# Keeping the four upper rows of a strip in place, and summing normalised tokens in GpSimd first

## What is computed

```python
# layer 0: windows of 8x8 queries against 12x12 keys (a halo of 2 pixels), 6 heads of 16
x = x + conv0(ln_c(x))            # qkv (1x1), scores + relative positions, softmax, P V, projection
t = tokens(x); t = t + ffn0(ln_t(t))        # 96 -> 384 -> 96, rounded to 8-bit floats
# layer 1: clusters in each of 8 quadrants (2 batches x 2 x 2), 4 heads of 24, 2 x 2 centres
x = x + conv1(ln_c(x))
#   centres = mean of the features over each of 2 x 2 parts of a quadrant
#   sim = sigmoid(beta + alpha * cosine(centre, point)), the best centre only
#   agg = (sum_n sim * value + value centre) / (sum_n sim + 1); out = agg * sim
t = tokens(x); t = t + ffn1(ln_t(t))
```

## Time and profile before

| | |
|---|---|
| time, median of 3 runs | 9565.71 us (9555.72 to 9568.57) |
| the profiled execution, its own time | 9573.13 us |
| its span in the trace | 9571.3 us |
| PE busy | 8344.2 us (87%) |
| DVE busy | 7322.2 us (77%) |
| ACT busy | 4988.4 us (52%) |
| POOL busy | 2176.8 us (23%) |
| chain that ended last: PE, DVE, ACT | 59%, 26%, 6% of the span |
| granted clock of PE, mean | 0.905 of full speed |

### The profile page before, as it was taken

The page is one execution under the profiler, slowest core; times in us unless marked ns, Lnnn a source line. Parts: engine busy times, 40 slices in busy tenths (PEclk is TensorE's granted clock), DMA queues, the critical chain, the costliest instruction groups (busy, mean ns, idle before and its releaser), DMA issues.

```text
span 9571.3 us, 441216 instructions
## 1 busy us (share of the span) xinstructions
PE 8344.2 (87%) x175538; PEld 6638.7 (69%) x175538; DVE 7322.2 (77%) x24166; ACT 4988.4 (52%) x9994; POOL 2176.8 (23%) x4356
## 2 busy tenths in 40 slices
PE   8999999998888888888888888988888989888665
PEld 6777777777767767777777766776777777776443
DVE  5777777778787777787777778777778778877666
ACT  3555445445555555555555555555555555555445
POOL 2323222222222222222222222222222222222000
PEclk9999999999999999999999999999999999998555
DMA  2111112112122122222222212222222222221111
GB/s 59 49 45 46 49 49 52 50 47 60 53 58 59 53 56 59 55 58 57 55 54 59 56 51 58 58 55 54 60 55 55 60 55 54 60 55 50 57 57 61
DMA packets 191968, 525.03 MB, mean 55 GB/s; under 512 B 33372, under 2 KB 66972, under 8 KB 189980
## 3 DMA queue, kind: packets, MB, share of 16 engines
q1 hardware_dynamic: 190204, 498.89, 19.3%
HBM read 252.61 MB, written 168.30 MB: 44 GB/s over the span
## 4 chain that ended last, share of the span: by engine, by line
PE 59%; DVE 26%; issue 8%; ACT 6%; DVEq 1%; SPq 0%; ACTq 0%; DMA 0%; POOL 0%; POOLq 0%
PE scores_x L644 10%; PE flipped L666 6%; PE bank L551 5%; PE misc L560 4%; PE pv L694 3%; PE bank L614 3%; PE bank L912 3%; DVE maxes L1510 3%; PE pv L688 3%; PE scores_x L585 2%; DVE z L1625 2%; PE bank L939 2%; PE pv L895 2%; PE bank L621 2%; DVE shifted L1518 2%
## 5 line engine op out<-in xcount | busy, mean ns | idle before, releaser
L1510 DVE TENSOR_REDUCE maxes<-scores_x 128x6 f32<-128x864 f32 x1024 | 1079.1, 1054 | 1046.3 <-PE scores_x L644 973.6
L1957 POOL TENSOR_TENSOR vrest<-vstage,vmask 96x384 f32<-96x384 f32 x512 | 431.5, 843 | 5592.6 <-ACT vstage L1141 5592.6
L644 PE MATMUL scores_x<-keys,queries 64*64 64x144 f32 x24576 | 1101.4, 313 | 436.6 <-DVE shifted L1518 414.8
L644 PEld LDWEIGHTS scores_x<-keys,queries 64*64 64x64 f32 x24576 | 803.8, 144 | 678.0 <-issue 627.9
L1179 ACT ACTIVATE probs<-flipped 128x384 f32<-128x384 f32 x1024 | 497.6, 486 | 1320.1 <-PE flipped L666 1320.1
L1518 DVE TENSOR_TENSOR shifted<-scores_x,maxes 128x768 f32<-128x768 f32 x1024 | 970.2, 948 | 0.0
L606 PE MATMUL bank<-xn,wq 97*32 97x64 f32 x24576 | 869.4, 221 | 56.7 <-issue 56.0
L666 PE MATMUL flipped<-ident,shifted 128*128 128x128 f32 x6144 | 918.6, 289 | 0.1
L603 PE MATMUL bank<-xt,wq 97*32 97x64 f32 x24576 | 846.6, 221 | 65.3 <-issue 51.0
L603 PEld LDWEIGHTS bank<-xt,wq 97*32 97x32 f32 x24576 | 727.7, 110 | 248.7 <-issue 224.8
L1129 ACT ACTIVATE queries<-bank 128x512 f32<-128x512 f32 x768 | 458.6, 597 | 835.6 <-PE bank L606 835.6
(11 more groups left out here) (185 smaller groups left out, 18387.2 us busy)
## 6 DMA issues: line engine op xcount, KB each, us to landing
x_in<-x_dram SPq DMA_DIRECT2D x128, 594.0 KB
keys<-kst SPq DMA_DIRECT2D x768, 99.0 KB
xn_kept<-xn SPq DMA_DIRECT2D x128, 388.0 KB, 3.9
later<-xn_kept SPq DMA_DIRECT2D x128, 388.0 KB, 3.3
x_tok<-tok_dram SPq DMA_DIRECT2D x128, 384.0 KB, 3.5
x_kept<-x SPq DMA_DIRECT2D x128, 384.0 KB, 2.4
later<-x_kept SPq DMA_DIRECT2D x128, 384.0 KB, 3.7
out_dram<-later SPq DMA_DIRECT2D x128, 384.0 KB, 2.5
```

Source lines behind the costliest of these rows:

```text
L644: last = mm(score[e][64 * j:64 * j + 64, g * NKEY:(g + 1) * NKEY], queries[64 * e:64 * e + 64, g, w, :], keys[64 * e:64 * e + 64, g, :, WS ...
L1510: V.tensor_reduce(maxes[:, p % 2, :, :], sc, AX.X, ALU.max).then_inc(max_ready.sem, 1)
```

## The change

It has two parts.

**Four rows kept.** A strip now loads only the 8 rows that are new (1056 columns), in three chunks of 352, and everything from the mean to the keys is done on these: 3 means, 12 variance matmuls (stationary operands of 88 columns), 12 transposes, 3 key matmuls, 3 centrings, 3 normalisations, 3 squares and 3 stores of keys for each strip. The last four rows of `xn` and of `kst` (528 columns each) are copied by POOL to their first four rows (`keep_halo`), once the queries, windows and keys of the strip have been taken. The quadrants of a column now follow each other (b, c, r), so that 32 strips hang together; there are four column starts. Their upper rows are made at the program's start as two extra strips, -2 and -1, stored to DRAM, and loaded from there at each start (`store_tops`, `load_top`).

**Sum in two steps.** POOL adds the tiles of each half in two `tensor_tensor` instructions (388 and 194 columns), and PE's `pool` is 2 matmuls in place of 8.

```diff
+TOP = 2 * HALO * PADW
+NEW = WS * PADW
+CH = NEW // 3
+COLUMN = FOLD * STRIPS
+STARTS = BATCH * FOLD
-        x_in = sb("x_in", [128, KW, PADW])
+        x_in = sb("x_in", [128, WS, PADW])
+        xn2_half = sb("xn2_half", [128, 2, 2, PROW])
+        xn2_sum = sb("xn2_sum", [128, 2, PROW])
+        xn_new = xn_flat[:, TOP:STRIP]
...
             def load_keys(n):
-                sp.wait_ge(k_stored.sem, k_stored.at(n, 4))
+                sp.wait_ge(k_stored.sem, k_stored.at(n, 3))
+                sp.wait_ge(halo_ready.sem, halo_ready.at(n, 2))
...
+            load_x(-2)
+            load_x(-1)
+            store_tops(0)
             load_x(0)
+            store_tops(1)
             load_x(1)
+            load_top(0)
...
                     if p == 1 and ahead:
                         mean(n + 1, 2)
-                        mean(n + 1, 3)
...
                     if p == 3 and ahead:
                         variance(n + 1, 2, on)
-                        variance(n + 1, 3, on)
...
                     if p == 7:
                         if ahead:
                             spread(n + 1, 2)
-                            spread(n + 1, 3)
...
                     make_queries(n + 1, 0, on)
                     make_keys(n + 1, 2)
                     make_queries(n + 1, 1, on)
-                    make_keys(n + 1, 3)
...
             def pool(n, at=SUMS):
-                pe.wait_ge(xn2_ready.sem, xn2_ready.at(n, 1))
+                pe.wait_ge(xn2_summed.sem, xn2_summed.at(n, 2))
                 for u in range(2):
-                    for j in range(4):
-                        last = mm(pv[0:PROW, at + u:at + u + 1], xn2[:, 4 * u + j, :], pool_w[:, :],
-                                  start=(j == 0), stop=(j == 3), skip_group_check=True)
+                    last = mm(pv[0:PROW, at + u:at + u + 1], xn2_sum[:, u, :], pool_w[:, :],
+                              start=True, stop=True, skip_group_check=True)
...
             def centre_x(n, c):
                 if c == 0:
-                    dve.wait_ge(q_ready.sem, q_ready.at(n, 0))
-                    dve.wait_ge(win_ready.sem, win_ready.at(n, 0))
-                    dve.wait_ge(xt_ready.sem, xt_ready.at(n, 0))
+                    if not isinstance(n, int) or n > 0:
+                        dve.wait_ge(halo_ready.sem, halo_ready.at(n, 1))
...
+                by_half = xn2[:, :, :].rearrange("p (u a b) c -> p u a b c", u=2, a=2)
+                P.tensor_tensor(xn2_half[:, :, :, :], by_half[:, :, 0], by_half[:, :, 1], ALU.add
+                                ).then_inc(xn2_summed.sem, 1)
+                pool.wait_ge(xn2_summed.sem, xn2_summed.at(n, 1))
+                P.tensor_tensor(xn2_sum[:, :, :], xn2_half[:, :, 0, :], xn2_half[:, :, 1, :], ALU.add
+                                ).then_inc(xn2_summed.sem, 1)
+
+            def keep_halo(n):
+                pool.wait_ge(q_ready.sem, q_ready.at(n, 6))
+                pool.wait_ge(win_ready.sem, win_ready.at(n, 4))
+                P.tensor_copy(xn_flat[0:PROW, 0:TOP], xn_flat[0:PROW, NEW:STRIP]
+                              ).then_inc(halo_ready.sem, 1)
+                pool.wait_ge(k_loaded, n * (16 * NH) + 16 * NH)
+                P.tensor_copy(kst[0:C, 0:TOP], kst[0:C, NEW:STRIP]).then_inc(halo_ready.sem, 1)
...
                 mask_values(n, 0)
                 repeat_rest(n, 2)
+                if column:
+                    take_top(column)
+                elif on.ahead:
+                    keep_halo(n)
                 if on.b2:
                     normalise_stream(n - 2)
                 mask_values(n, 1)
```

More of the change, by code:

```diff
@@ L190, in build @@
         simw = sb("simw", [128, TILES, SW])
-        squares = [kst[0:C, c * CH:(c + 1) * CH] for c in range(4)]
+        squares = [kst[0:C, TOP + c * CH:TOP + (c + 1) * CH] for c in range(3)]
         a0, a1 = 2 * TILES * C, 2 * TILES * C + 2 * TILES * PROW
@@ L451, in store_out, with strip @@
                              ).then_inc(out_stored, 16)
-            def strip(n, par, on):
+            def strip(n, par, on, column=0):
+                if column:
+                    load_top(column)
                 load_residual(n)
@@ L496, in _ @@
                 strip(n, n % 2, stage(n))
-            with sp.Fori(0, STRIPS // 2 - 2) as s:
+            with sp.Fori(0, STRIPS // 2 - 3) as s:
                 for par in range(2):
                     strip(2 * s + (LAG_B + 2 + par), par, stage(LAG_B + 2))
+            strip(COLUMN - 2, 0, stage(COLUMN - 2))
+            strip(COLUMN - 1, 1, stage(COLUMN - 1), 1)
             for n in range(LAG_C - 2, LAG_C + 2):
                 strip(n, n % 2, stage(n))
-            with sp.Fori(0, (N - 4 - LAG_C) // 2) as s:
-                for par in range(2):
-                    strip(2 * s + (LAG_C + 2 + par), par, stage(LAG_C + 2))
+            for j in range(2, STARTS + 1):
+                first = max((j - 1) * COLUMN, LAG_C + 2)
+                with sp.Fori(0, (j * COLUMN - 2 - first) // 2) as s:
+                    for par in range(2):
+                        strip(2 * s + (first + par), par, stage(LAG_C + 2))
+                if j < STARTS:
+                    strip(j * COLUMN - 2, 0, stage(LAG_C + 2))
+                    strip(j * COLUMN - 1, 1, stage(LAG_C + 2), j)
             for n in range(N - 2, N):
@@ L1067, in _ @@
             setup()
-            for c in range(4):
-                mean(0, c)
-            for c in range(4):
-                variance(0, c)
-            for c in range(4):
-                spread(0, c)
-            for c in range(4):
-                make_keys(0, c)
+            for n in (-2, -1, 0):
+                if n > -2:
+                    pe.wait_ge(k_stored.sem, k_stored.at(n, 0))
+                for c in range(3):
+                    mean(n, c)
+                for c in range(3):
+                    variance(n, c)
+                for c in range(3):
+                    spread(n, c)
+                for c in range(3):
+                    make_keys(n, c)
             for i in range(6):
@@ L1359, in _ @@
             setup()
-            for c in range(4):
-                square(0, c)
-            for c in range(4):
-                store_keys(0, c)
+            for n in (-2, -1, 0):
+                for c in range(3):
+                    square(n, c)
+                for c in range(3):
+                    store_keys(n, c)
             for i in range(6):
@@ L1871, in _ @@
             setup()
-            for c in range(4):
-                centre_x(0, c)
-            variance(0)
-            dve.wait_ge(newton_x.sem, newton_x.at(0, 1))
-            rsqrt(rs_a_chain, 0, VT, 16, newton_x, 1, [(0, 16, rs_y[0:VT, 0:16], rstd_x)])
-            for c in range(4):
-                normalise_x(0, c)
+            for n in (-2, -1, 0):
+                for c in range(3):
+                    centre_x(n, c)
+                variance(n)
+                dve.wait_ge(newton_x.sem, newton_x.at(n, 1))
+                rsqrt(rs_a_chain, n, VT, 12, newton_x, 1, [(0, 12, rs_y[0:VT, 0:12], rstd_x)])
+                for c in range(3):
+                    normalise_x(n, c)
             for n in range(2):
@@ L1990, in _ @@
             strip(2, stage(2))
-            with pool.Fori(3, N - 1) as n:
-                strip(n, stage(3))
+            for j in range(1, STARTS + 1):
+                with pool.Fori(max((j - 1) * COLUMN, 3), j * COLUMN - 1) as n:
+                    strip(n, stage(3))
+                if j < STARTS:
+                    strip(j * COLUMN - 1, stage(3), j)
             strip(N - 1, stage(N - 1))
@@ L2099 @@
                                 ("sims_kept", TILES * SW))]
+    kept += [nc.dram_tensor(name, (2, rows, NEW), F32, kind="Internal").ap()
+             for name, rows in (("top_xn", PROW), ("top_keys", C))]
     build(nc, x_ap, tok_ap, aps, o_ap, *kept)
```

157 lines of the change are left out of this document (107 added, 50 removed).

## The result

The changed kernel takes **9187.06 us** (median of four runs, 9184.59 to 9189.38) against 9567.14 us of the kernel before (four runs, 9555.72 to 9581.88): ratio 0.9602, 95% interval 0.9585 to 0.9618, or 4.0% less. The forecast was 9203 us in a range from 9080 to 9390. The profiled execution took 9189.38 us, with a span of 9187.4.

What follows compares the result with a forecast made beforehand. PE's path through each strip, then DVE's tail, was taken as the bound. Savings of 263 (third stage), 79 (first) and 56 us (second), less 35 for the start, took the profiled 9573 to 9210, forecast as 9203 us; range 9080 to 9390.

Steps and rivals of the forecast that it cites:

- 1.47 becomes 0.37, saved 1.10: Pooled sum on PE's path: two matmuls of eight remain, saving 1.10 us a strip.
- Means 2 and 3, 0.83: Second pair of means on PE's path: 1.50 us becomes 0.67, saving 0.83 a strip.
- Variances 0 and 1, 0.16: First eight variance matmuls on PE's path, with narrower stationary operands: 0.16 us of 1.49 saved a strip.
- ACT and DVE don't take the path: Against the rival that they keep half the third stage's gain (232 us saved, 9334 us; chance 0.16).
- the low clock goes: Rival: fewer one-column matmuls spare PE's fall to 1.2 GHz, 1 us a strip, 94 us, giving 9110; chance 0.14.
- 2.88 x 0.11 = 0.32: Means 0 and 1 in the third stage, at the low clock: narrower chunks save 0.32 us a strip.
- 1.50 x 0.11 = 0.17: Means 0 and 1 in the first stage, at the full clock: narrower chunks save 0.17 us a strip.
- its 4.4: First stage's net gain a strip: 4.9 us saved on PE's path less 0.5 for POOL's copies.
- I take 0.7 a strip: DVE time lost to POOL's halo copies in the tail, second and third stage: 0.7 us, within 0 to 2.4.
- in full: Rival: both halo copies block DVE's chain, 2.4 us a strip, leaving 142 us saved, 9424 us; chance 0.12.
- A store to DRAM that must land adds 3 or so: Each of two starting strips: some 14 us of work plus 3 for the store; 35 us allowed together.
- signs of being wrong: Copy over 1.2 us, new POOL wait, third-stage strip 71 us or more, start over 50 us longer, third-stage clock moved over 0.01.

Runs made afterwards that it cites:

- halo-only run: Changed kernel with POOL's two additions removed and pooling again by eight matmuls, the kept rows staying: 9326.16 us, ratio 0.9736 to the kernel before.
- all one-column matmuls back: Changed kernel with four unread variance matmuls added and pooling again by eight matmuls without POOL's additions: 9442.55 us.
- run with the store cut: Changed kernel with each starting store of normalised rows split from 97 partitions into 96 and 1: 9158.71 us.
- filler: Changed kernel with six dense, unread matmuls given to PE ahead of the scores of pair 1: 9128.48 us.
- the sum alone: Kernel before with only the two-step sum (POOL adds, PE pools with two matmuls), no kept rows: 9460.28 us, ratio 0.9877.
- run with all three edits: Changed kernel with starting stores split, halo copies behind POOL's normalisation from strip 32, and six unread matmuls in the third stage only: 9002.38 us, ratio 0.9417.

## Why the prediction was right, and where its terms were not

The forecast is 16 us above the time measured, and the measured time lies inside the range and on the side forecast, but that is partly the work of errors that cancel. Without the clock's gain of some 101 us, which the forecast did not count, the time would have been about 9288 us: still inside the range, and 85 us off in place of 16.

- **What held.** The sum in two steps, "1.47 becomes 0.37, saved 1.10": 1.03 in section 6, 139 us by the halo-only run. Means 2 and 3, 0.83: measured 0.70 and 0.78. Variances 0 and 1, 0.16: measured 0.16 and 0.21. That the additions cost nothing, and that POOL is in time: no wait for it grew. That ACT and DVE don't take the path: with a mean or four variances put back nearly the whole of their length comes back (79 and 102 us, 0.6 and 0.8 a strip), so PE bounded those sections. That the other column starts cost nothing: POOL waits there for the loaded rows (27.9 us in all), but strips 31, 63 and 95, in which it does, are shorter than before by 3.3 us on the mean, much as the others.
- **The clock, which the forecast had put aside.** The rival "the low clock goes" gave 1 us a strip at one chance in seven. It came, in the place named and at nearly the price named (1.1 us a strip, 94 strips, about 105 us). That the price fits is luck in part: the rival had 1.38 us in two of three strips, and it was 2.48 us in 46 of 100. The reason it gave does not hold in the third stage: with all one-column matmuls back the clock holds; with mean and variances back it falls again in 30 of 100 strips.
- **The head of the strip.** "2.88 x 0.11 = 0.32" and "1.50 x 0.11 = 0.17" became 0.12 saved in the third stage and 0.89 lost in the first. There PE is at the low clock for more than 1 us in sections 0 and 1 in 8 of the 15 strips from 2 to 16, and was in one; scores at 1.64 and means at 2.32 are its price. It came in 4 of 15 in the run with the store cut (51.88 us a strip), so its size is not firm, and no run was made for it. The runs with the kept rows and no filler have it in 4 to 10 of 15, the sum alone in 3, so it seems to come with the kept rows; why is open. With the filler ahead of it, it came in one. It is the larger half of the 1.65 us by which the first stage missed its 4.4; the rest is the tail, where 0.75 came of 1.8 less 0.5. (With the halo alone this tail stays at 22.52 us, where the kernel before has 22.55; what of the 0.75 is the kept rows' is not shown.)
- **The ports.** "I take 0.7 a strip": the tail grew by 0.33 net of the shorter keys and transposes (0.25), so about 0.6. Doubling the copies says 0.6 as well, moving them 0.8 in the tail. Of the 0.6 the eleven small steps show 0.33 (2.81 before, 3.14 now); where the rest lies is not shown. The copy itself took 0.62 us for the 0.8 taken. The rival "in full" had 1.20 for each copy, twice. Here a step beside each copy stands 0.33 and 0.30 us longer than its 0.17, and the normalisation that stood in their place before had slowed the same steps too, which the forecast had named.
- **The start.** "A store to DRAM that must land adds 3 or so" is the term that was most wrong: 18.3 us, twice. The start cost 50 us for 35; with the store cut it costs 28. The term took a store of 97 partitions for one like any other.

Against the forecast, then: the clock won 1.07 x 94 = 101 us and the tail of the third stage 0.12 x 94 = 11; the head lost 0.20 x 94 = 19 and sections 2 and 6 another 0.20 x 94 = 19; the first stage lost 1.65 x 18 = 30 and the start 15, while the second won 0.17 x 16 = 3. That makes 32 us more than the 363 forecast; the profiled executions have 384, 21 more. The rest, 11 us, is the drain (1.5 longer) and the strips that the means leave out.

Of the forecast's own signs of being wrong none came, but two stand at their edge: the start is longer by 50.0 us, where over 50 was the sign, and the granted clock of the third stage went from 0.925 to 0.933 (shown as 0.92 and 0.93), where more than 0.01 was. A copy takes 0.62 us, and a third-stage strip 68.5 for the 69 named; the first stage has 52.3 for 51.

## What to carry to other kernels

Work that is moved to GpSimd is not free because GpSimd is idle: look at what VectorE does in the same microseconds, and put the move behind its chain of small dependent steps; here this order was worth 84 us. Do not let a transfer that somebody waits for span 97 partitions: cut into 96 and 1 it ran here at ten times the rate. And a gain on TensorE should be priced section by section at the clock that it has there, since this change moved the clock in two places that it was not meant for, by more than some of the terms themselves.

## What the runs showed of the hardware that I had not expected

- A store of 97 partitions x 4.2 KB kept DVE waiting for 18.3 us and held back the 96-partition one behind it (14.8 us from issue to landing, and 3.0 with the cut); cut into 96 and 1 no wait for it is left.
- In the kernel before, PE's clock falls to 1.2 GHz late in a strip although PE has hardly any idle time there (busy for 9.87 of 10 us in strips that keep 2.4 GHz, 10.00 in those that don't). In the changed kernel it is busy for 8.6 to 9.5 of 10 us there and the clock holds in every strip. Which of the two is cause, if either, is open.
- Six matmuls without use made a third-stage strip 1.05 us shorter. PE's timeline of the run with all three edits has them at 4.04 us:

```profile
5057.03 4.04 PE L792 MATMUL flipped<-wq,wk 97*96 97x384 f32 x12
```

- Three small DVE steps, which take some 0.17 us alone, took 1.00, 0.52 and 0.55 us: the first met two POOL instructions, the others one each. The Trainium skill (SBUF — State Buffer, "Who interferes with whom") has the loser of the shared ports wait for the whole instruction. The trace agrees, with ends within 0.06 us of POOL's.
